# Five side-by-side parts per lane in two row scans, and record clearing moved to the edge layer

## The chip, the core and the metric

The kernel runs on one core of a Trainium2 chip. The metric is the device time of one execution in microseconds, here the median of three runs. The engines are named as in the profile: PE (TensorE), DVE (VectorE), ACT (ScalarE), POOL (GpSimd) and SP (SyncE, which only issues transfers in this kernel).

## What is computed

Four graph layers over 12,500 nodes of 64 features and 400,000 edges, sorted by target node `dst`. Each is `x = x + layer(relu(layernorm(x)))`:

```python
# 0, the edge layer
x_i = x[dst]; x_j = x[src]
h = relu(concat([x_i, x_j - x_i]) @ W1 + b1)
out = segment_max(h @ W2 + b2, dst)          # 0 for a node without edges
# 1: leaky_relu(segment_sum((x * norm_src)[src], dst) * norm_dst @ W + b)
# 2: two hops of a mean over neighbours, each with a matmul of [own, mean]
# 3, the last layer: every edge's row has a weight of its own
message = x[col] * edge_weight[:, None]      # col = dst, row = src
neigh_agg = segment_sum(message, row)
x @ W_self.T + b_self + neigh_agg @ W_neigh.T + b_neigh
```

## The kernel before

**Layout.** The 400,000 sorted edges are split into 128 lanes, one for each partition, of `LANE` = 3125 edges that follow each other. A lane is walked in 125 blocks of `K` = 25 edges. Buffers of five slots (`R` = 5) hold five blocks, and one turn of a hardware loop handles five.

**Edge layer** (the loops over `body0`, from 619 us to 8264 us of the span). For each block:

- SP loads the indices of a later block (`index_load`, line 642), the keys (lines 649 to 651) and the block's rows of `first_rows` (`load_fill`, line 939). `first_rows` has a node's row where its first edge stands, and zeros elsewhere. SP does so in `pass_index` when the block before has been scanned (semaphore `scanned`).
- POOL gathers `x_j` rows with 25 indirect transfers (line 636), one for each column of the block, 128 rows each. It waits for the indices alone and is four to five blocks ahead of DVE.
- DVE makes one-hot matrices of keys (line 685, 20 a block, of which 16 come in pairs for `v` = 0 to 7, the others before them), for PE's counting products. Between them stand single steps of two scans over the 25 columns, each column 128x64 (line 1395, `scan_steps`). The **fill** repeats a node's row over its edges: `fill[j] = fill[j-1]*keep + fill[j]`. The **max** scan takes the running maximum: `ring[j] = max(min(ring[j-1], mask), product[j])`, with the product in a PSUM bank of eight columns. Each step of a scan waits for the one before it. The fill of block b+1 goes on beside the max of block b. After the scan comes the sum of gathered and filled rows (line 1426).
- PE turns the block's rows (line 1928), multiplies them by the second weight (line 1953, semaphore `products0`), and does the counting products (line 1898): first `hist_counts`, 25 pairs of matmuls with no wait among them, then 16 a `v`.
- ACT copies the turned rows and the counts out of PSUM (lines 1755, 1739), and issues the stores of counts (784 KB) and edge rows (800 KB) of the block.

**Three dense sums** (`dense_*`, layers 1 and 2) multiply the stored counts with the nodes' rows, 31 groups each. Beside each group but the first, ACT issues a store of zeros to `records`, the last layer's table (88 stores of 1960 KB, 173 MB in all).

**Last layer** (`body4`, 12,049 us to about 16,775 us), for each of 125 blocks:

- DVE copies the masks (line 691), runs the fill scan over 25 columns, now from SBUF into PSUM banks (line 1630), works out where each message goes in `records` (lines 1638 to 1652), and splits the messages into bf16 planes with ACT (lines 1657, 1662). It then gives `targets`.
- ACT multiplies each filled column by the edge's weight (line 1835) and makes the high and middle planes (1839, 1844). It writes into one of three message buffers, once the scatters that read it last are done.
- PE adds up 25 one-hot matrices for the next block's positions (line 1898, tile kp).
- POOL scatters the 25 columns of messages (line 1181), 128 rows each. It waits for `targets`.
- SP loads first rows, keys and weights five blocks ahead (lines 939 and 1092).

Then 220 units read `records` back and sum them, and the output is written. Small pieces stand between the stages: `place_nodes` works out each node's first and last edge, `first_rows_gpsimd` scatters nodes' rows to `first_rows` and reads one row for each lane's first edge, and `fix_vector`/`fix_gpsimd` carry the maximum over lane borders.

## Time and profile before

| | us |
|---|---|
| median of 3 runs (lowest, highest) | 17606.11 (17545.68, 17622.48) |
| the profiled execution | 17562.39 |
| its span | 17560.6 |
| edge layer's blocks, 619 to 8264 | 7645 |
| last layer's blocks, 12,049 to 16,775 | 4726 |

Busy shares of the span are 44% for PE, 51% for DVE, 34% for ACT and 41% for POOL. No engine is busy throughout, so what a stage costs must be read from that stage. The profiled execution stands 44 us under the median. In a trace row, the first number is the start in us, the second the duration in us, and square brackets hold the idle time of that engine ahead of the row and what ended it.

### The profile page before, as it was taken

The numbers are of one execution on the slowest core, as the hardware profiler recorded it, in microseconds if no ns is written. First come the engines' busy times: TensorE is split into PE (matmuls) and PEld (weight loads), VectorE is DVE, ScalarE is ACT, GpSimd is POOL, SyncE is SP. The second block draws the span as 40 slices with busy tenths as digits, with TensorE's granted clock in tenths as the row PEclk, the third lists the DMA queues.
The fourth block names the chain that finished last, engine by engine and source line by source line (L and its number), as shares of the span: only waits on it lengthen the run. The fifth ranks groups of instructions, "written<-read, shape, count | busy, mean of one in ns | idle before, by whom it ended". The sixth has DMA issues, their size and how long they took to land. (4 is left out here: it accounts for less than half of the span.)

```text
span 17560.6 us, 235099 instructions
## 1 busy us (share of the span) xinstructions
PE 7737.4 (44%) x71916; PEld 5437.9 (31%) x71916; DVE 9024.9 (51%) x17849; ACT 5959.3 (34%) x10705; POOL 7168.5 (41%) x7069
## 2 busy tenths in 40 slices
PE   1244444444444444444697999992000000000045
PEld 1233333333333333333354555551000000000045
DVE  4355555555555555556444443434555555555565
ACT  0122222222222222222576777772222222222211
POOL 4434334343443433333211111115666666666610
PEclk9755555555555555555898998995555555555588
DMA  7222222222222222222585886881111111111177
GB/s 279 89 69 69 69 69 73 66 73 71 69 69 69 69 69 69 69 69 76 183 264 188 253 264 194 262 255 55 56 54 57 55 56 55 57 57 57 51 251 242
DMA packets 1287056, 1982.88 MB, mean 113 GB/s; under 512 B 257381, under 2 KB 1004742, under 8 KB 1281561
## 3 DMA queue, kind: packets, MB, share of 16 engines
q1 hardware_dynamic: 886377, 1080.50, 20.1%
q10 hardware_dynamic: 174288, 612.09, 9.2%
q0 software_dynamic: 225664, 281.41, 5.7%
q8 instruction: 358, 5.87, 0.1%
q14 instruction: 369, 3.02, 0.1%
HBM read 1171.31 MB, written 815.77 MB: 113 GB/s over the span
## 5 line engine op out<-in xcount | busy, mean ns | idle before, releaser
L636 POOL DMA_INDIRECT RF<-tab_edge_b,idx x3125 | 3076.1, 984 | 4638.8 <-DMA idx<-e_src 3636.2
L685 DVE TENSOR_TENSOR HM<-iota_b,eqw 128x2048 bf16<-128x2048 bf16 x2000 | 2192.3, 1096 | 3318.4 <-remote 2902.3
L1181 POOL DMA_INDIRECT records<-RF,idx x3125 | 3094.3, 990 | 1678.8 <-issue 1064.8
L1898 PE MATMUL bk<-HM 128*128 128x98 bf16 x16000 | 1642.8, 254 | 2720.0 <-ACT X L1739 1176.6
L1739 ACT ACTIVATE X<-bk 128x392 uint8<-128x392 f32 x4000 | 1779.8, 495 | 1504.9 <-PE bk L1898 1438.2
L1898 PE MATMUL kp<-HM,ident_b 128*128 128x98 bf16 x3125 | 275.2, 282 | 4473.6 <-issue 2420.2
L1898 PEld LDWEIGHTS bk<-HM 128*128 128x128 bf16 x16000 | 1152.7, 119 | 3253.2 <-issue 3170.6
L769 PE MATMUL tp<-HM,RF 128*64 128x512 bf16 x12276 | 1977.4, 379 | 4.2 <-ACT HM L728 2.6
L876 POOL DMA_INDIRECT agg<-RF,lastT x372 | 537.5, 1445 | 2887.7 <-ACT RF L808 2796.9
L1898 PEld LDWEIGHTS kp<-HM,ident_b 128*128 128x128 bf16 x3125 | 251.6, 142 | 4498.1 <-issue 4498.1
L1755 ACT ACTIVATE hT<-tp 128x512 f32<-128x512 f32 x500 | 255.7, 511 | 3619.2 <-remote 2939.6
L775 PE MATMUL om<-HM,RF 128*64 128x512 bf16 x6138 | 1326.3, 379 | 0.0
L769 PE MATMUL tp<-RF 128*64 128x512 bf16 x5952 | 1011.3, 381 | 226.9 <-ACT RF L728 226.9
L1953 PE MATMUL om<-w_diag,hT 128*128 128x128 f32 (+1 forms) x3250 | 846.5, 400 | 442.0 <-issue 434.5
L769 PEld LDWEIGHTS tp<-HM,RF 128*64 128x64 bf16 x12276 | 813.7, 110 | 632.1 <-issue 72.4
L1395 DVE SCALAR_TENSOR_TENSOR RF<-RF,dupjunk 128x64 f32<-128x64 f32 x3124 | 876.8, 281 | 27.3
L1953 PEld LDWEIGHTS om<-w_diag,hT 128*128 128x128 f32 (+1 forms) x3250 | 711.2, 298 | 535.2 <-issue 510.7
L1395 DVE SCALAR_TENSOR_TENSOR RF<-RF,dupjunk,om 128x64 f32<-128x64 f32 x3124 | 860.4, 275 | 0.4
L730 DVE CAST HM<-dst_f 128x4096 bf16<-128x4096 uint8 x186 | 427.0, 2296 | 727.3 <-DMA dst_f<-counts 401.1
L1630 DVE SCALAR_TENSOR_TENSOR tp<-tp,mblk,RF 128x64 f32<-128x64 f32 x1875 | 549.0, 293 | 468.5 <-DVE tp L1630 255.2
L728 ACT ACTIVATE RF<-dst_f 128x4096 bf16<-128x4096 uint8 x186 | 672.7, 3617 | 331.7 <-PE tp L769 330.6
L728 ACT ACTIVATE HM<-dst_f 128x4096 bf16<-128x4096 uint8 (+1 forms) x186 | 702.2, 3822 | 46.6 <-PE tp L769 46.6
(362 smaller groups left out, 14990.4 us busy)
## 6 DMA issues: line engine op xcount, KB each, us to landing
dst_f<-counts SPq DMA_DIRECT2D x465, 512.0 KB
RF<-first_rows SPq DMA_DIRECT2D x250, 800.0 KB
counts<-X ACTq DMA_DIRECT2D x250, 784.0 KB
records<-RF ACTq DMA_DIRECT2D x88, 1960.0 KB
RF<-records SPq DMA_DIRECT2D x220, 784.0 KB, 5.0
crow<-counts SPq DMA_DIRECT2D x279, 512.0 KB
first_rows<-RF ACTq DMA_DIRECT2D x25, 4000.0 KB
edge_rows<-RF ACTq DMA_DIRECT2D x125, 800.0 KB
```

The costliest lines, as they stand in the source:

```text
L636: e.indirect_dma_start(out=ring[:, r, j, :], out_offset=None, in_=table[:, :], in_offset=bass.IndirectOffsetOnAxis(ap=idx[:, r, j:j + 1], ...
L685: return e.tensor_tensor(to[:, 0:n, :].rearrange("p k (q h) -> p k q h", h=2), iota_b[:, 0:m].rearrange("p (q h) -> p q h", h=2).unsqueeze ...
L728: e.activation(to, of, ACT.Copy).then_inc(sem("widened_A"), 1)
L769: last = e.matmul(tp[u][k * D:(k + 1) * D, :], hi_mid[:, t, k * D:(k + 1) * D], part, start=t == 0, stop=t == TILES - 1, skip_group_check= ...
L775: return e.matmul(om[u][k * D:(k + 1) * D, :], low[:, t, :], part, start=t < 2, stop=t >= TILES - 2, skip_group_check=True)
L876: e.indirect_dma_start(out=agg[:, :], out_offset=bass.IndirectOffsetOnAxis(ap=lastT[:, g * GB + k:g * GB + k + 1], axis=0), in_=out_rows[g ...
L1181: e.indirect_dma_start(out=records[:, :], out_offset=bass.IndirectOffsetOnAxis(ap=idx2[:, r, j:j + 1], axis=0), in_=msgs[MSG_OF[r]][:, j, ...
L1395: e.scalar_tensor_tensor(out=buf[:, r, j, :], in0=prev, scalar=mask[:, j:j + 1], in1=this, op0=op0, op1=op1).then_inc(sem(chain.name), 1)
L1630: loop_chain(e.scalar_tensor_tensor(out=in_bank(j), in0=prev, scalar=mblk[:, 0, j:j + 1], in1=fill[:, r, j, :], op0=ALU.mult, op1=ALU.add))
L1739: e.activation(staged[u].rearrange("p (r k) -> p r k", k=P)[:, :, k:k + 4], bk[s % 2][:, 0:4 * TILES].rearrange("p (k r) -> p r k", k=4), ...
L1898: return e.matmul(to, by_q, by_r, start=start, stop=stop, skip_group_check=True)
L1953: last = e.matmul(om[q % 2][:, k * P:k * P + m], hT[0:m, q % 2, k * P:(k + 1) * P], w_diag[0:m, 0:m], start=True, stop=True)
```

## The change

**Parts.** Each lane's 3125 edges are seen as five parts (`VL` = 5) of 625, and a block now takes five columns of each part in place of 25 columns that follow each other. Position `c*5 + v` of a block is column c of part v, so the five rows of one `c` belong to five separate walks. One instruction of 320 elements does a scan step for five positions:

```python
# fill, in the edge layer and, with mblk, in the last layer
e.copy_predicated(columns(fill, r, c), bcast(mask c), earlier_columns(fill, r, c))
# max
e.scalar_tensor_tensor(out=kept, in0=earlier_columns(ring, r, c), scalar=1.0,
                       in1=bcast(mask), op0=ALU.mult, op1=ALU.min)
e.tensor_tensor(ring[:, r, a:z, :], kept[...], om[q % 2][...], ALU.max)   # a piece per PSUM bank
```

A fill of a block is 5 instructions (25 before), a max is 5 + 8 (25 before; the pieces end where a bank of eight columns ends). In the last layer the fill stays in SBUF, and ACT reads it there:

```diff
-                    for q, cols in enumerate(FILLQ):
-                        wait(e, "highs", b * NF + (q + 1 - NF + 3 * NGROUPS))
...
-                        for j in cols:
-                            prev = in_bank(j - 1) if j else in_bank(K - 1)
...
-                            loop_chain(e.scalar_tensor_tensor(out=in_bank(j), in0=prev, scalar=mblk[:, 0, j:j + 1],
-                                                              in1=fill[:, r, j, :], op0=ALU.mult, op1=ALU.add))
...
+                    for c in range(JJ):
+                        if not (isinstance(b, int) and b + c == 0):
+                            loop_chain(e.copy_predicated(columns(fill, r, c), bcast(mblk[:, 0, c * VL:(c + 1) * VL].bitcast(i32)),
+                                                         earlier_columns(fill, r, c)))
...
-                            last = e.activation(msg_bank(q)[:, j - cols[0], :], in_bank(j), ACT.Copy, scale=wblk[:, r, j:j + 1])
+                            last = e.activation(msg_bank(q)[:, j - cols[0], :], fill[:, r, j, :], ACT.Copy, scale=wblk[:, r, own(j):own(j) + 1])
```

SP's load of a later fill slot in the last layer now also waits for `filled4` of the next block, which reads the slot's last five columns.

**Order on DVE in the edge layer.** The waits for `products0` move from ahead of a pair of one-hots to the first instruction that reads the bank, and the fill and max steps are spread anew:

```diff
                 for h in range(2):
                     for _ in hist_batch(b, h):
-                        several(filling, 2)
+                        several(filling, 1)
                 for _ in count_batch(b, r, 0):
-                    several(filling, 2)
-                for q, cols in enumerate(MAXQ):
-                    wait(e, "products0", b * NQ + (q + 1))
-                    gate(e)
-                    taking = scan_steps(max_chain, ring, b, r, masks[:, r, 1, :], ALU.min, ALU.max, cols, om[q % 2])
-                    for v in range(2 * q + 1, min(2 * q + 3, VB)):
-                        for _ in count_batch(b, r, v):
-                            several(taking, 1)
-                            several(filling, 1)
-                            several(taking, 1)
...
+                    several(filling, 1)
+                taking = max_steps(b, r)
+                for v in range(1, VB):
+                    for _ in count_batch(b, r, v):
+                        several(taking, 1)
+                several(taking, K)
```

**Loads in runs of five.** The indices, and in the last layer the keys and weights, lie in five runs of five numbers (20 bytes) a lane, not in one run of 25 (100 bytes):

```diff
-            e.dma_start(idx[:, r, :], src_l[:, bass.ds((i * R + r) * K, K)])\
+            e.dma_start(by_part(idx[:, r, :]), by_part(src_l)[:, :, bass.ds((i * R + r) * JJ, JJ)])\
...
-                        e.dma_start(to[:, r, :], of[:, bass.ds(b * K, K)]).then_inc(sem(f"first{r}"), 16)
+                        e.dma_start(by_part(to[:, r, :]), by_part(of)[:, :, bass.ds(b * JJ, JJ)]).then_inc(sem(f"first{r}"), 16)
```

**Clearing.** The stores of zeros leave ACT's dense groups. SP issues them behind each block's loads in the edge layer, 120 of 128x10x280 numbers (1400 KB) and four of 128x8x280:

```diff
                 for r in range(R):
                     pass_index(e, i, r)
                     load_fill(e, 0, i, r)
+                    clear_records(e, (i * R + (r - R)) * CLEAR_ROWS + (R - 1) * CLEAR_FIRST, CLEAR_ROWS)
...
-                if not isinstance(g, int) or g > (0 if l == 0 else 1):
-                    e.dma_start(records_flat.rearrange("(p c w) -> p c w", p=P, w=CLEAR_COLS)
...
```

**Small pieces.** `row_numbers` turns edge numbers into the new row order (7 operations on 128x98, called twice). The row for a lane's start and the repair at borders are done for five parts: five indirect transfers where one stood (twice in `first_rows_gpsimd`, twice in `fix_gpsimd`), and 12 more short DVE operations in `fix_vector`.

**DVE's order in the edge layer**, from the first one-hots of a `v` with its fill and max steps. RF holds the ring and the fill, dupjunk the masks, om the products, eqw the keys, HM the one-hots. Before:

```order
L685 TENSOR_TENSOR HM<-iota_b,eqw 128x2048 [waits products0,histed]
L1395 SCALAR_TENSOR_TENSOR RF<-zero_row,dupjunk,om 128x64
L1395 SCALAR_TENSOR_TENSOR RF<-RF,dupjunk 128x64 [waits v_fill]
L1395 SCALAR_TENSOR_TENSOR RF<-RF,dupjunk,om 128x64 [waits v_max]
L685 TENSOR_TENSOR HM<-iota_b,eqw 128x1568
L1395 SCALAR_TENSOR_TENSOR RF<-RF,dupjunk,om 128x64 [waits v_max]
L1395 SCALAR_TENSOR_TENSOR RF<-RF,dupjunk 128x64 [waits v_fill]
L1395 SCALAR_TENSOR_TENSOR RF<-RF,dupjunk,om 128x64 [waits v_max]
```

The same place in the changed kernel (pivots is the buffer of `kept`):

```order
L698 TENSOR_TENSOR HM<-iota_b,eqw 128x2048 [waits histed]
L1473 SCALAR_TENSOR_TENSOR pivots<-RF,dupjunk 128x320
L698 TENSOR_TENSOR HM<-iota_b,eqw 128x1568
L1486 TENSOR_TENSOR RF<-pivots,om 128x320 [waits products0,v_max]
L698 TENSOR_TENSOR HM<-iota_b,eqw 128x2048 [waits banked]
L1473 SCALAR_TENSOR_TENSOR pivots<-RF,dupjunk 128x320 [waits v_max]
L698 TENSOR_TENSOR HM<-iota_b,eqw 128x1568
L1486 TENSOR_TENSOR RF<-pivots,om 128x192 [waits v_max]
```

Behind each one-hot stood three steps of two scans, and now stands one of one scan; the wait for the products is one one-hot pair later.

**DVE's order in the last layer**, from a block's masks to the positions. Before:

```order
L691 COPY mblk<-keep 128x25
L1630 SCALAR_TENSOR_TENSOR tp<-tail,mblk,RF 128x64 [waits v_loop,first1,highs]
L1630 SCALAR_TENSOR_TENSOR tp<-tp,mblk,RF 128x64 [waits v_loop] x7
L1630 SCALAR_TENSOR_TENSOR tp<-tp,mblk,RF 128x64 [waits v_loop,highs]
L1630 SCALAR_TENSOR_TENSOR tp<-tp,mblk,RF 128x64 [waits v_loop] x7
L1630 SCALAR_TENSOR_TENSOR om<-tp,mblk,RF 128x64 [waits v_loop,highs]
L1630 SCALAR_TENSOR_TENSOR om<-om,mblk,RF 128x64 [waits v_loop] x7
L1630 SCALAR_TENSOR_TENSOR tail<-om,mblk,RF 128x64 [waits v_loop,highs]
L1638 CAST rtwice<-rblk 128x50 [waits v_loop]
```

In the changed kernel:

```order
L1699 COPY_PREDICATED RF<-mblk,RF 128x320 [waits v_loop,first1]
L1699 COPY_PREDICATED RF<-mblk,RF 128x320 [waits v_loop] x4
L1707 CAST rtwice<-rblk 128x50 [waits v_loop]
L1710 TENSOR_TENSOR hT<-rtwice 128x625 [waits v_loop]
L1712 TENSOR_TENSOR hT<-hT,eqw 128x625 [waits v_loop]
```

A chain of 25 dependent instructions with four waits for ACT has become a chain of five with none.

**SP's order in the edge layer**, one block of the loop in the changed kernel:

```order
L655 DMA idx<-e_src 128x5x5
L661 ISA
L661 TENSOR_LOAD chunk
L661 ISA x2
L662 ISA
L662 DMA crow<-kr 128x256
L663 ISA
L663 DMA rel<-rel_lin 128x128
...
L958 DMA RF<-first_rows 128x1600
L1010 ISA
L1010 DMA records<-pivots 128x10x280
```

The index load keeps its place and has five runs a lane; the store of zeros stands last.

## Rows read from the trace of the kernel before

**Rows 1.** Busy time by stretch: us, PE, PEld, DVE, ACT, POOL, clock, DMA share, GB/s.
```profile
619.00:8264.00 7645.00, 3603.20 (x27859) 2783.10 (x27859) 4112.70 (x9473) 2074.73 (x4621) 2990.03 (x3038) 0.57 0.22 69
8480.00:9512.00 1032.00, 1027.93 (x9326) 580.42 (x9322) 417.67 (x215) 807.41 (x276) 172.93 (x120) 1.00 0.83 259
12049.00:16775.00 4726.00, 274.21 (x3115) 250.80 (x3116) 2594.97 (x5240) 1177.68 (x4246) 3070.15 (x3100) 0.50 0.18 55
```
**Rows 2.** Timeline of POOL, one block's gathers and the next block's first.
```profile
4003.49 0.95 POOL L636 DMA_INDIRECT RF<-tab_edge_b,idx  x1 [29.65 <-DMA idx<-e_src]
...
4033.80 0.94 POOL L636 DMA_INDIRECT RF<-tab_edge_b,idx  x1 [0.30 <-issue]
4067.97 0.94 POOL L636 DMA_INDIRECT RF<-tab_edge_b,idx  x1 [33.22 <-DMA idx<-e_src]
```
**Rows 3.** Timeline of PE in that block: counting pairs and turns.
```profile
4014.42 0.25 PE L1898 MATMUL mixed<-HM,ident_b 128*128 128x98 bf16 x1
...
4038.87 0.37 PE L1928 MATMUL tp<-ident,RF 128*128 128x128 f32 x1 [0.84 <-issue]
```
**Rows 4.** Timeline of DVE in that block.
```profile
4039.09 1.23 DVE L685 TENSOR_TENSOR HM<-iota_b,eqw 128x2048 bf16<-128x2048 bf16 x1 [24.88 <-remote]
4040.23 0.60 DVE L1395 SCALAR_TENSOR_TENSOR RF<-RF,dupjunk 128x64 f32<-128x64 f32 x2
4040.75 0.97 DVE L685 TENSOR_TENSOR HM<-iota_b,eqw 128x1568 bf16<-128x1568 bf16 x1
...
4043.49 0.28 DVE L1395 SCALAR_TENSOR_TENSOR RF<-RF,dupjunk,om 128x64 f32<-128x64 f32 x1
...
4044.07 0.97 DVE L685 TENSOR_TENSOR HM<-iota_b,eqw 128x1568 bf16<-128x1568 bf16 x1
```
**Rows 5.** Timeline of DVE, the sums of the last two blocks, behind the last gather.
```profile
8195.60 1.82 DVE L1426 TENSOR_TENSOR RF<-RF 128x1600 f32<-128x1600 f32 x1
8230.65 1.82 DVE L1426 TENSOR_TENSOR RF<-RF 128x1600 f32<-128x1600 f32 x1
```
**Rows 6.** Busy time by stretch, inside the block of rows 2.
```profile
4006.00:4016.00 10.00, 6.38 (x48) 5.37 (x49) 6.10 (x16) 1.09 (x2) 7.87 (x8) 0.57 0.94 342
4018.00:4034.00 16.00, 2.67 (x11) 1.05 (x10) 0.00 (x0) 0.00 (x0) 12.04 (x14) 0.50 0.12 27
```
**Rows 7.** Groups of instructions by line and shape: busy us, mean ns.
```profile
L431 DVE SCALAR_TENSOR_TENSOR HM<-HM,stat_rstd 128x448 f32<-128x448 f32 x56 | 35.0, 625 | 7.9 <-remote 2.8 <-DVE stat_rstd L430 2.8 <-issue 0.6
L1524 DVE COPY_PREDICATED X<-HM 128x448 f32<-128x448 int32 x14 | 9.2, 657 | 2.0 <-DVE HM L1523 0.8 <-issue 0.8
L1657 DVE TENSOR_TENSOR om<-om,RF 128x512 f32<-128x512 f32 x125 | 87.4, 700 | 29.4 <-issue 21.7 <-DVE idx L1652 7.7
```
**Rows 8.** DMA issues: count, KB each, median us to landing.
```profile
idx<-e_src SPq DMA_DIRECT2D x125, 12.5 KB, 1.7
RF<-records SPq DMA_DIRECT2D x220, 784.0 KB, 5.0
```
**Rows 9.** Timeline of DVE in the last layer, a block with quick fill steps.
```profile
13593.35 2.71 DVE L1647 TENSOR_TENSOR HM<-HM,kp 128x2450 f32<-128x2450 bf16 x1
13604.35 0.34 DVE L1630 SCALAR_TENSOR_TENSOR tp<-tail,mblk,RF 128x64 f32<-128x64 f32 x1 [0.37 <-DVE mblk L691]
...
13613.61 0.20 DVE L1638 CAST rtwice<-rblk 128x50 bf16<-128x50 f32 x1 [0.24 <-issue]
13617.67 2.71 DVE L1647 TENSOR_TENSOR HM<-HM,kp 128x2450 f32<-128x2450 bf16 x1
```
**Rows 10.** The same, the block before it, with slow fill steps.
```profile
13556.62 0.29 DVE L1630 SCALAR_TENSOR_TENSOR tp<-tail,mblk,RF 128x64 f32<-128x64 f32 x1 [0.97 <-DVE mblk L691]
...
13584.86 0.20 DVE L1638 CAST rtwice<-rblk 128x50 bf16<-128x50 f32 x1 [1.81 <-issue]
```
**Rows 11.** Line 1647 in all: duration ns min/median/max, first and last start.
```profile
L1647 DVE TENSOR_TENSOR HM<-HM,kp x125: 2707/2707/2708, 12062.8 to 16770.9; 128x2450 f32<-128x2450 bf16 x125
```
**Rows 12.** POOL's scatters, group by line: busy us, mean ns of one, idle before.
```profile
L1181 POOL DMA_INDIRECT records<-RF,idx x3125 | 3094.3, 990 | 1678.8 <-issue 1064.8 <-DVEq L329 614.0
```

More of the change, by code:

```diff
@@ L22 @@
 BLOCKS = LANE // K
+VL = 5
+JJ = K // VL
+VLEN = LANE // VL
+ROUND = 1.5 * 2.0 ** 23
 ITERS = BLOCKS // R
@@ L49 @@
 RW = 98
[L50 removed]
+CLEAR_COLS, CLEAR_ROWS, CLEAR_FIRST = 280, 10, 8
 MSG_OF = (0, 1, 2, 0, 1)
@@ L886, in fix_tensor, with fix_vector @@
             e.transpose(pb[:, 0:D], carryT[:, 0:P], ident[0:D, 0:D]).then_inc(sem("fix_tensor"), 1)
-        def fix_vector(e, chain, l, op0, op1, row, colc):
-            e.tensor_copy(tail[:, :], ring[:, R - 1, K - 1, :]).then_inc(sem("fix_vector"), 1)
+        def fix_vector(e, chain):
+            last = lambda v: ring[:, R - 1, K - VL + v, :]
+            for v in range(1, VL):
+                chain(e.scalar_tensor_tensor(out=tail[:, :], in0=tail[:, :] if v > 1 else last(0),
+                                             scalar=part["kL"][:, v:v + 1], in1=last(v), op0=ALU.min, op1=ALU.max))
+            e.sem_inc(sem("fix_vector"), 1)
@@ new lines, in fix_vector @@
+            for v in range(1, VL):
+                chain(e.scalar_tensor_tensor(out=carried[:, v, :], in0=carried[:, v - 1, :], scalar=part["kL"][:, v - 1:v],
+                                             in1=last(v - 1), op0=ALU.min, op1=ALU.max))
+            e.wait_ge(sem("fix_read"), 16 * VL)
+            for v in range(VL):
+                chain(e.scalar_tensor_tensor(out=fixrow[:, v, :], in0=carried[:, v, :], scalar=part["contL"][:, v:v + 1],
+                                             in1=fixrow[:, v, :], op0=ALU.min, op1=ALU.max))
@@ L1067, in _ @@
                 load_fill(e, 0, 0, r)
+            e.wait_ge(sem("zero_tile"), 1)
+            for r in range(R - 1):
+                clear_records(e, r * CLEAR_FIRST, CLEAR_FIRST)
             with e.Fori(1, ITERS) as i:
@@ new lines, in _ @@
+            chain(e.tensor_tensor(part["cont"][:, :], part_starts, part["prev"][:, :], ALU.is_equal))
+            chain(e.tensor_scalar(part["whole"][:, :], part["cnt"][:, :], float(VLEN), None, ALU.is_equal))
+            chain(e.tensor_tensor(part["whole"][:, :], part["whole"][:, :], part["cont"][:, :], ALU.mult))
+            chain(e.tensor_tensor(col["k"][:, :], part["whole"][:, 0:1], part["whole"][:, 1:2], ALU.mult))
+            for v in range(2, VL):
+                chain(e.tensor_tensor(col["k"][:, :], col["k"][:, :], part["whole"][:, v:v + 1], ALU.mult))
```

234 lines of the change are left out of this document (139 added, 95 removed).

## The prediction

> **What bounds the kernel now.** I read the busy time by stretch first, then the timelines of single blocks, since no engine is busy throughout [rows 1]. Three stages matter, and each has a limit of its own.
>
> *Edge layer.* 7645 us for 125 blocks are 61.2 us a block, and no engine is busy for 60% of it [rows 1]. POOL's gathers start at 4003.49 and the last is issued at 4033.80, a burst of 30.3 us; the next burst starts at 4067.97, after 33.22 us of waiting for indices, which SP loads only when DVE has scanned a block [rows 2]. So POOL waits for DVE. DVE in turn waited 24.88 us, up to 4039.09, for PE and ACT [rows 4]. PE was within its 25 counting pairs at 4014.42 and needed until 4038.87 for the rest and the block's turn, though nothing that it waited for shows [rows 3]. In 16 us it started 11 matmuls, while the transfers kept only 12% of the DMA engines busy [rows 6]. What I call **slow issue** is this: the engine is free, its data is there, and instructions come one by one, about 16 / 11 = 1.5 us apart. It ends about 5 us after POOL's last gather, with the turn at 4038.87. Behind the last burst there is none, and a block takes 8230.65 - 8195.60 = 35.05 us, not 61 [rows 5]. A block is thus a front as long as POOL's burst and some 5 us, set off by the index load, and a back of some 25 us that DVE mostly bounds.
>
> *Dense sums.* PE is busy for 1027.93 of 1032 us at full clock [rows 1].
>
> *Last layer.* A block takes (16770.9 - 12062.8) / 124 = 37.97 us [rows 11]. It is made of two sorts of block. With quick steps it takes 24.32 us from one line 1647 to the next, of which the fill takes 13613.61 - 13604.35 = 9.26 us [rows 9]. In the block before, the same fill took 28.24 us, 13556.62 to 13584.86 [rows 10]: slow issue again, beside POOL's scatters. POOL itself needs 25 x (0.990 + 0.30) = 32.2 us a block and was idle for 1678.8 us [rows 12]; 0.30 us of that idle time stands before each scatter.
>
> **The change part by part.** The sum is against the profiled execution, 17562 us.
>
> *Last layer's fill: -590 us.* 25 dependent steps go, 5 come. A predicated copy of 448 elements takes 657 ns, a step of 64 about 290 ns [rows 7, 9]; by the line between them, 320 elements take 535 ns, and with 0.03 us between them five take 2.8 us. A quick block falls from 24.3 to 24.3 - 9.3 + 2.8 = 17.8 us. In a slow block I charge each step the pace of the slow ones, 28.24 / 25 = 1.13 us, on top of little work of its own, so at most 5 x (1.13 + 0.25) = 7 us in place of 28. Such a block takes some 46 us now and would take 25. Both are under POOL's 32.2 us, so POOL becomes the bound, and DVE waits for it instead (through ACT, which waits for a message buffer). Bounds: 32.2 us a block, -5.8 x 125 = -720 us; and nothing, if slow issue spreads over all blocks once POOL never rests. I take 33.2 us, near POOL's floor, because either sort of block is well under it: -4.75 x 125 = -594 us. ACT's 25 weightings now read SBUF; ACT is busy for 1177.68 / 125 = 9.4 us a block in all [rows 1], so even at twice that it lies beside POOL's 32.
>
> *Edge layer's scans: -375 us.* In the back of a block stood 4 fill steps in pairs, 0.52 us a pair (4040.23 to 4040.75), and 14 groups of a max, a fill and a max, each 4044.07 - 4043.49 = 0.58 us [rows 4]: 1.04 + 8.1 = 9.1 us. The other eight fills lie in the front, which is hidden. Now the back has one fill (0.45 us), five minimum steps and eight maximum pieces. The step of 448 elements takes 625 ns, and one of 512 with PSUM 700 ns [rows 7]. Scaled to 320 and with the overlap of 0.09 us that successive rows show [rows 4], five are 5 x 0.40 = 2.0 us; the pieces cover 1600 elements in all, 1600/512 x 0.61 + some 0.06 x 8 = 2.4 us. That is 4.9 us, so DVE saves 4.2 us. PE and ACT work in step with DVE there, through the banks of counts, and may be close behind it, so I take 3.0 us of it; bounds 1 and 4.2, that is -125 to -525 us.
>
> *Index load: +200 us.* It has 640 runs of 20 bytes and not 128 of 100, and every block's front starts with it. It lands 1.7 us after issue; 784 KB in 512 runs land in 5.0 us [rows 8]. At the 342 GB/s of a busy stretch [rows 6] the bytes of the latter are 2.3 us, so 384 more runs cost 1.0 us, and 512 more 1.3 us; small runs are less even, so I take 1.7 us x 120 = 204 us. Bounds: 0, and all of 3.3 us for 384 runs, 4.4 us for 512, 530 us. The Trainium skill ("DMA: Bandwidth & Descriptors", Measured) gives about 10.5 ns for each packet as a floor; by that 512 more are 5.4 us, and the sum would be 440 us worse. The trace speaks against so much, since 512 runs with 784 KB of data land within 5.0 us in all, and no row here has a load of 640 runs.
>
> *Clearing in the edge layer: +0 us.* 1.43 MB more a block are 4.2 us at 342 GB/s [rows 6]. They are issued last by SP, behind the index load, and the busy stretch of transfers ends near 4016 today, 18 us ahead of POOL's last gather [rows 2, 6]. That burst is the cover; if the stores hold up the gathers' data or the fetch of instructions by their whole length, they cost 4.2 x 124 = 520 us. A gain cannot be excluded: PE's slow issue might start later.
>
> *Clearing out of the dense sums: 0 us.* PE waits for nothing there [rows 1].
>
> *Small pieces: +25 us.* 16 more indirect transfers at 1.29 us [rows 12] are 21 us; some 35 short DVE operations at 0.2 to 0.3 us are 9 us, part of it beside other work. Bounds 10 and 50 us.
>
> Sum: -594 - 375 + 204 + 25 = -740 us, so 16,822 us for the profiled execution. It stood 44 us under the median; I forecast **16,870 us** for the median.
>
> **The rivals.**
>
> *Slow issue takes the last layer's gain.* It seems tied to POOL's work, and a POOL that never rests leaves no quick blocks. PE's 25 pairs, ACT's 50 instructions and DVE's remaining 20 all need issue. For it: in a slow block 25 steps took three times their time. Against it: the parts of the block with long operations, from line 1647 to the fill, take about as long in slow blocks. If a block keeps 36.5 us, the last layer gives 185 us and the total is 17,230 us. If in addition the index load costs its upper bound, nothing is left of it: 17,560 us, no change.
>
> *The edge layer's front grows (slower).* The index load and the stores of zeros both lengthen the front, which every block pays. Without an other change, (594 + 375 - 25) / 125 = 7.6 us more a block eat all gains. At the upper bounds, 4.4 + 4.2 = 8.6 us; should the stores also stretch slow issue by as much again, 12.8 us. That is 17,560 + 5.2 x 125 = 18,210 us, at the middle of this case 17,900. The share of 94% of the DMA engines in the first 10 us [rows 6] speaks for it; the quiet 18 us behind it speak against.
>
> *Slow issue in the edge layer gives way.* If it starts 4 us later because bulk transfers last 4 us longer, PE has done its counting before it, and the front no longer needs the burst's end. A block could fall towards the 35.05 us of rows 5, at most to POOL's 32 us. A fifth of that way, 5 us, gives 16,240 us; half of it 15,250 us. Nothing in the rows shows why it starts, so I can't exclude it.
>
> *The change does little:* the counts of instructions are as stated, but DVE isn't what the back waits for, and ACT or PE is. Then the edge layer loses 200 us by the index load and the last layer pays for it only in part: 17,500 us.
>
> **How the numbers follow.** Chances: forecast 0.50; slow issue takes the gain 0.17 (of it 0.12 at 17,230 and 0.05 at no change); front grows 0.15 (0.02 of it within 0.5%); edge layer gives way 0.10; little effect 0.08. A measurement of this kernel can tell about 0.5%, 88 us, from no change. Faster by more: 0.50 + 0.12 + 0.10 + 0.02 = 0.74. Within: 0.05 + 0.02 + 0.06 = 0.13. Slower: 0.13. The range of the forecast itself comes from its bounds, 16,500 to 17,250. To leave out no more than 2 in 10 it takes in part of the second and the fourth case: 16,300 to 17,450.
>
> **What would show it.** In the last layer: line 1699 at some 0.53 us, POOL's scatters with little idle time but the 0.30 us, line 1717 each 33 us. In the edge layer: blocks of about 59.5 us; index load landing in 3 to 3.5 us; the wait before the first one-hot of `v` = 0 still over 20 us; the minimum step at 0.49 us. In the dense sums: 33 us a group as now, with a lower DMA share. The forecast is wrong if the last layer's blocks stay over 36 us, if edge blocks are longer than 61.2 us, or if the wait of 24.88 us has gone.

## The result, and the profile after

| | before | changed |
|---|---|---|
| median, us | 17603.28 (4 runs, 17545.68 to 17622.48) | 16603.31 (4 runs, 16570.32 to 16657.12) |
| ratio | | 0.9438, 95% interval 0.9411 to 0.9465 |
| profiled execution | 17562.39 | 16657.12 |

The change saves 1000 us in the median, and 905 us between the two profiled executions, since the profiled one before lies 41 us under its median and the one after 54 us over it. The forecast was 16,870 us with a range from 16,300 to 17,450, so the time lies in the range, 267 us under the forecast. Its two large terms are both wrong, though, and they err in opposite directions. That shows as soon as the profile is read stage by stage.

Busy time by stretch of the changed kernel, edge layer and last layer (columns, and the rows of the kernel before: [rows 1]):

```profile
619.00:7440.00 6821.00, 3311.91 (x27859) 2687.39 (x27859) 3655.90 (x5496) 2108.01 (x4620) 3159.39 (x3047) 0.60 0.33 104
11200.00:15840.00 4640.00, 275.16 (x3125) 251.59 (x3125) 2037.35 (x2742) 1252.41 (x4247) 3054.31 (x3087) 0.50 0.21 57
```

The sum that ends each edge block (first row; before: 619.3 to 8230.6) and the step that marks each last-layer block (second row; before: [rows 11]), first and last start:

```profile
L1506 DVE TENSOR_TENSOR RF<-RF x125: 1814/1818/1822, 624.9 to 7411.2; 128x1600 f32<-128x1600 f32 x125
L1717 DVE TENSOR_TENSOR HM<-HM,kp x125: 2706/2707/2708, 11215.9 to 15832.7; 128x2450 f32<-128x2450 bf16 x125
```

From these starts every piece of the span follows:

| piece | before | changed | difference |
|---|---|---|---|
| up to the first edge block | 619.3 | 624.9 | +6 |
| edge layer, 124 blocks | 7611.3 (61.4 a block) | 6786.3 (54.7 a block) | -825 |
| between (dense sums) | 3832.2 | 3804.7 | -27 |
| last layer, 124 blocks | 4708.1 (38.0 a block) | 4616.8 (37.2 a block) | -91 |
| to the end of the span | 789.7 | 822.7 | +33 |
| sum | 17560.6 | 16655.4 | -905 |

The forecast had -375 + 204 = -171 us for the edge layer and -594 us for the last one.

**Last layer.** Groups of DVE and POOL in the stretch from 11,200 to 15,840 us: the fill, the one-hot that follows it, the scatters.

```profile
L1699 DVE COPY_PREDICATED RF<-mblk,RF 128x320 f32<-128x320 int32 x624 | 325.1, 521 | 86.6 <-DMA wblk<-e_weight 18.6 <-issue 12.8 <-DVE mblk L704 10.4
L698 DVE TENSOR_TENSOR HM<-iota_b,rtwice 128x2450 bf16<-128x2450 bf16 x125 | 179.4, 1435 | 1685.3 <-remote 1639.7 <-issue 37.0 <-DVE inrank L1713 8.4
L1208 POOL DMA_INDIRECT records<-RF,idx x3086 | 3054.1, 990 | 1585.6 <-issue 979.0 <-DVEq L338 606.6
```

The same groups of the kernel before, from 12,049 to 16,775 us (the fill's two largest, the one-hot, the scatters):

```profile
L1630 DVE SCALAR_TENSOR_TENSOR tp<-tp,mblk,RF 128x64 f32<-128x64 f32 x1875 | 549.0, 293 | 468.5 <-DVE tp L1630 255.2 <-issue 114.8 <-remote 38.5
L1630 DVE SCALAR_TENSOR_TENSOR om<-om,mblk,RF 128x64 f32<-128x64 f32 x875 | 256.2, 293 | 505.8 <-DVE om L1630 359.9 <-issue 92.2 <-remote 33.1
...
L685 DVE TENSOR_TENSOR HM<-iota_b,rtwice 128x2450 bf16<-128x2450 bf16 x125 | 179.4, 1435 | 452.1 <-remote 303.2 <-issue 138.7 <-DVE inrank L1643 10.1
...
L1181 POOL DMA_INDIRECT records<-RF,idx x3100 | 3070.1, 990 | 1657.7 <-issue 1057.5 <-DVEq L329 600.1
```

The fill did what was forecast: 521 ns a step (535 was said), and DVE's busy time in the stage fell from 2595 to 2037 us. The idle time ahead of the fill steps is nearly gone: the two groups shown had 974 us of it, and now there are 87. A quick block fell to 18 us, as forecast (17.8). But the idle time ahead of one single instruction, the one-hot behind the fill, went from 452 to 1685 us, 1233 more. POOL stayed idle for nearly as long as before. A stall that had been spread over 25 steps now stands in one place.

The timelines of DVE, PE and POOL show what that place is like:

```profile
13523.68 2.94 DVE L1699 COPY_PREDICATED RF<-mblk,RF 128x320 f32<-128x320 int32 x5 [0.17 <-DVE mblk L704]
...
13528.46 0.81 DVE L1713 TENSOR_REDUCE inrank<-hT 128x25 f32<-128x625 bf16 x1
13572.11 1.44 DVE L698 TENSOR_TENSOR HM<-iota_b,rtwice 128x2450 bf16<-128x2450 bf16 x1 [42.84 <-remote]
...
13507.44 2.20 PE L1969 MATMUL kp<-HM,ident_b 128*128 128x98 bf16 x25 [22.17 <-issue]
13576.49 2.20 PE L1969 MATMUL kp<-HM,ident_b 128*128 128x98 bf16 x25 [66.84 <-DVEq L1718]
...
13568.57 0.97 POOL L1208 DMA_INDIRECT records<-RF,idx  x1 [0.30 <-issue]
```

The one-hot waits for PE's count, which PE makes from what DVE did in the block before. The row of PE's 25 products for it ends at 13509.64, 20 us before DVE came to the wait, and PE did nothing after it. DVE still stood for 42.84 us, until 3.5 us behind the start of the last of POOL's 75 scatters in a row (13568.57; the run of 75 began at 13473.17). Blocks now come mostly in threes of 18, some 25 and 69 us, where most took 24 or some 48 us before. Nor is it a late transfer of instructions: in these 40 us the trace has none, and in the 16 quiet us of [rows 6] none either. In the 69 us block SP's three small loads, between which it waits for nothing, go out 2.9 us apart:

```profile
13533.93 0.70 SPq L1119 DMA_DIRECT2D rblk<-r_lin  x1
13536.85 0.70 SPq L1119 DMA_DIRECT2D qblk<-q_lin  x1
13539.76 0.70 SPq L1119 DMA_DIRECT2D wblk<-e_weight  x1
```

**Edge layer.** Here is where a block's time goes, averaged over 105 blocks of each trace (worked out from the starts of the rows, not a view of the profile), in us from the start of the block's sum (line 1426, now 1506):

```
                                     before  changed
POOL's first gather                    1.9     2.5
POOL's last gather (25th)             32.8    34.8
first one-hot of v = 0                25.5    12.5
                     1                38.1    17.1
                     2                41.5    30.7
                     3                45.3    39.9
                     7                59.4    52.5
the next block's sum                  62.0    55.1
```

Before, v = 1 started 5.3 us behind POOL's last gather. Now v = 3 starts 5.1 us behind it. Two more values of `v`, each 3.55 us before (v = 1 to v = 7 in six steps), are started beside the burst. The five behind it take 3.15 us each in place of 3.55, 2.0 us in all. Against that the front is 2.0 us longer: 0.7 by the index load, 1.3 by slower gathers. -7.1 - 2.0 + 2.0 is -7.1 us, and the table has -6.9. It also shows that v = 0 starts 13 us sooner.

### The profile page after: what moved, and what is told of

Read it like the earlier page. It is cut to its first block and busy times, and to the rows that moved or that the text cites. A ratio compares the mean times of both kernels' runs of the same rounds, so it can differ in the third digit from the quotient of the medians.

```text
span 16655.4 us, 228031 instructions
## 1 busy us (share of the span) xinstructions
PE 7442.4 (45%) x71916; PEld 5270.8 (32%) x71916; DVE 8010.3 (48%) x11391; ACT 6068.0 (36%) x10705; POOL 7332.9 (44%) x7085
## 5 line engine op out<-in xcount | busy, mean ns | idle before, releaser
L645 POOL DMA_INDIRECT RF<-tab_edge_b,idx x3125 | 3236.0, 1036 | 3666.1 <-DMA idx<-e_src 2659.8
L698 DVE TENSOR_TENSOR HM<-iota_b,eqw 128x2048 bf16<-128x2048 bf16 x2000 | 2192.1, 1097 | 2833.1 <-remote 1632.3
L788 PE MATMUL om<-HM,RF 128*64 128x512 bf16 x6138 | 1451.4, 379 | 0.0
L782 PEld LDWEIGHTS tp<-HM,RF 128*64 128x64 bf16 x12276 | 857.1, 110 | 651.7 <-issue 49.0
L698 DVE TENSOR_TENSOR HM<-iota_b,rtwice 128x2450 bf16<-128x2450 bf16 x125 | 179.4, 1435 | 1685.3 <-remote 1639.7
L2024 PE MATMUL om<-w_diag,hT 128*128 128x128 f32 (+1 forms) x3250 | 706.8, 377 | 62.4 <-issue 60.3
L788 PE MATMUL om<-RF 128*64 128x512 bf16 x2976 | 726.5, 381 | 0.0
L741 ACT ACTIVATE HM<-crow 128x4096 bf16<-128x4096 uint8 x186 | 670.4, 3604 | 0.0
L2024 PEld LDWEIGHTS om<-w_diag,hT 128*128 128x128 f32 (+1 forms) x3250 | 637.3, 284 | 93.9 <-issue 75.8
```

The lines of the kernel that those rows point to most:

```text
L645: e.indirect_dma_start(out=ring[:, r, j, :], out_offset=None, in_=table[:, :], in_offset=bass.IndirectOffsetOnAxis(ap=idx[:, r, own(j):own ...
L698: return e.tensor_tensor(to[:, 0:n, :].rearrange("p k (q h) -> p k q h", h=2), iota_b[:, 0:m].rearrange("p (q h) -> p q h", h=2).unsqueeze ...
L741: e.activation(to, of, ACT.Copy).then_inc(sem("widened_A"), 1)
L782: last = e.matmul(tp[u][k * D:(k + 1) * D, :], hi_mid[:, t, k * D:(k + 1) * D], part, start=t == 0, stop=t == TILES - 1, skip_group_check= ...
L788: return e.matmul(om[u][k * D:(k + 1) * D, :], low[:, t, :], part, start=t < 2, stop=t >= TILES - 2, skip_group_check=True)
L2024: last = e.matmul(om[q % 2][:, k * P:k * P + m], hT[0:m, q % 2, k * P:(k + 1) * P], w_diag[0:m, 0:m], start=True, stop=True)
```

## The experiments

The experiments ran on three chips, and that turned out to matter. A ratio is always to the kernel before on the same chip. The changed kernel itself stands beside the experiments on the third chip alone. On the first two its place is taken by the result above (ratio 0.9438, 54.7 and 37.2 us a block), whose own chip is not on record; the kernel before took 17603.28 us there, 17617.26 us on the first chip and 17534.60 us on the second.

### First chip: are the stores of zeros the cause?

With the change, bulk transfers last until about 16 us into POOL's burst and not 12, and slow issue (instructions that come one by one though nothing that they wait for is late) seemed to begin when they end. So theory A was that the stores hold it off.

**The stores moved back to the dense sums:**

```diff
-                    clear_records(e, (i * R + (r - R)) * CLEAR_ROWS + (R - 1) * CLEAR_FIRST, CLEAR_ROWS)
...
+                if not isinstance(g, int) or g > (0 if l == 0 else 1):
+                    clear_records(e, g * 14 + (-1, 28, 57)[l] * 14, 14)
```

> The changed kernel with the stores of zeros moved back: SP stores none in the edge layer, ACT stores 88 of 1960 KB beside the dense groups. The edge layer's block fell from 61.5 us to 55.0 us (medians) with the change. Theory A (transfers hold off slow issue: bulk transfers last until about 17 us into POOL's burst in place of 12, so DVE gets two more v into the front): without the stores the block goes back by the two v, 2 x 3.3 us, and the burst falls by 1 us, so 59 to 61 us a block, total 17,150 to 17,350 us. Theory B (the shorter scans and the wait behind the one-hots do it, the stores cost a little): block 54 us, total 16,450 to 16,600 us. The dense sums stay at 33 us a group in both.

Measured: 16638.62 us, ratio 0.9455 (0.9432 to 0.9477). The edge block takes (7384.4 - 623.5) / 124 = 54.5 us. The stretch between the layers takes 3805.6 us with the stores in it, 3804.7 without them. The block is where theory B had it (54), the total 39 us above its range.

**The same from the other side,** the kernel before with SP's stores in the edge layer, and none in the dense sums:

```diff
-                if not isinstance(g, int) or g > (0 if l == 0 else 1):
-                    e.dma_start(records_flat.rearrange("(p c w) -> p c w", p=P, w=CLEAR_COLS)
...
                     load_fill(e, 0, i, r)
+                    clear_records(e, (i * R + (r - R)) * 10 + (R - 1) * 8, 10)
```

> The kernel before with nothing changed but the stores of zeros: SP issues them behind each block's loads in the edge layer, ACT none in the dense sums. Theory A (transfers hold off slow issue): the pairs of the first counts are done before it starts, v = 0 and v = 1 move into the front; but DVE waits for the products ahead of v = 1 as before, so a part of the gain: block 57 to 59 us, total 17,050 to 17,300 us. Theory B (scans and wait do it): block 61.5 to 63 us, total 17,600 to 17,800 us.

Measured: 17627.04 us, ratio 1.0004 (0.9989 to 1.0019). In the profile the edge block is 60.5 us and not 61.4, and the last layer's 39.3 and not 38.0; the total shows neither. The last layer's code is the same in both, so between two profiles a stage can move by 1.3 us a block without an edit of its own. In this kernel v = 0 starts at 20.5 us, 5 us sooner than in the kernel before, so with the old scans the stores do move the front a little; v = 3 comes 1.2 us sooner. Neither theory's block (57 to 59, 61.5 to 63) was met.

**Twice the stores:**

```diff
                     clear_records(e, (i * R + (r - R)) * CLEAR_ROWS + (R - 1) * CLEAR_FIRST, CLEAR_ROWS)
+                    clear_spare(e, (i * R + (r - R)) * CLEAR_ROWS, CLEAR_ROWS)
```

> The changed kernel with a second store of zeros of 1400 KB behind each block's first in the edge layer, into a table that nothing reads. Theory A: bulk transfers last until about 21 us into the burst, DVE gets one or two more v into the front, block 50 to 53 us, total 16,000 to 16,350 us, unless POOL's burst grows by as much. Theory B: the block is the same or 1 to 4 us longer by the burst, total 16,600 to 17,100 us.

Measured: 16635.22 us, ratio 0.944 (0.9419 to 0.9461), edge block 54.6 us.

**Stores in the last layer:**

```diff
+                    if not isinstance(i, int):
+                        clear_spare(e, (i * R + (r - R)) * CLEAR_ROWS, CLEAR_ROWS)
             loop(e, body4)
```

> The changed kernel with a store of zeros of 1400 KB a block in the last layer, issued by SP behind the block's loads, into a table that nothing reads. The last layer's blocks take 37.2 us, in threes of 18, 24 and 69 us, with DVE waiting up to 42.8 us although what it waits for was done 20 us before. Theory A (bulk transfers hold off slow issue): at least half of the stall goes, blocks 33 to 35.5 us, total 16,100 to 16,400 us. Theory B (slow issue does not depend on bulk transfers, they only cost): blocks 37.2 to 41 us, total 16,600 to 17,100 us.

Measured: 16668.64 us, ratio 0.9456 (0.9417 to 0.9495), last-layer block 37.6 us.

Theory A asked for another time in each of the four, and in none did it come. In the totals, stores of 1400 KB a block cost nothing and give nothing that shows, in either layer, and neither do those of the dense sums. Clearing is worth 0 in both places, as forecast; the end of the bulk transfers does not set where the front ends.

### Second chip: the wait's place, SP's load, POOL's burst

**The wait for the products put back ahead of the one-hots:**

```diff
                 for v in range(1, VB):
+                    if v % 2:
+                        wait(e, "products0", b * NQ + (v + 1) // 2)
+                        gate(e)
                     for _ in count_batch(b, r, v):
```

> The changed kernel with DVE's wait for the products put back ahead of the one-hots of v = 1, 3, 5 and 7, where the kernel before has it; the new scans stay. Of 6.9 us a block that the edge layer gave, two v that DVE now does beside POOL's burst are 7.1, shorter steps about 2, and the longer burst takes 2. Theory W (the wait's place lets DVE go ahead): v = 1 goes back behind the burst, the block back to 58 to 61 us, total 17,000 to 17,350 us. Theory S (the shorter scans alone, with fewer instructions on DVE, do it): block 55 to 56.5 us, total 16,600 to 16,800 us.

**The kernel before with the later wait:**

```diff
-                    wait(e, "products0", b * NQ + (q + 1))
-                    gate(e)
-                    taking = scan_steps(...)
                     for v in range(2 * q + 1, min(2 * q + 3, VB)):
                         for _ in count_batch(b, r, v):
-                            several(taking, 1)
+                            done += 1
+                            if done == 2:
+                                wait(e, "products0", b * NQ + (q + 1))
+                                gate(e)
+                                taking = scan_steps(...)
+                            several(taking, 3)
```

> The kernel before with its old scans of 25 steps, but with DVE's wait for the products behind the one-hots of v = 1, 3, 5 and 7, and the eight maximum steps of a bank behind it in threes. Theory W (the wait's place): v = 1 and one more v in the front, block 56.5 to 59 us, total 17,000 to 17,300 us. Theory S (the scans): block 60.5 to 62 us, total 17,450 to 17,700 us.

**A small load in place of SP's 800 KB in the last layer:**

```diff
-                    load_fill(e, 4, i, r)
...
+                        wait(e, "filled4", i * R + (r - R + 2))
+                        gate(e)
+                        e.dma_start(fill[:, r, 0, :], lrows(first_rows)[:, bass.ds((i * R + r) * K, 1), :]
+                                    .rearrange("p a f -> p (a f)")).then_inc(sem(f"first{r}"), 16)
```

From the sixth block on the other 24 columns of the slot keep old rows, so this kernel scatters other messages and its output is another one.

> The changed kernel, but in the last layer SP loads only the first of a block's 25 columns of first_rows, 32 KB in place of 800 (from the sixth block on; the rest of the slot keeps old rows, so the messages are other ones). In the trace slow issue seemed to begin where SP issues this load. Theory L (the load sets slow issue off): the blocks fall from 37.2 us to 32.5 to 34 us, total 16,000 to 16,250 us. Theory P (slow issue comes with POOL's long bursts of scatters, whatever SP does): blocks 36.5 to 37.5 us, total 16,500 to 16,650 us.

**POOL waits for its scatters behind each block:**

```diff
+                    wait(e, f"moved{r}", i * (16 * K) + (16 * ITERS * K + 16 * K))
+                    gate(e)
             loop(e, body4)
```

> The changed kernel, but in the last layer POOL waits behind each block's 25 scatters until they have landed, 2 to 3 us, before it goes on to the next block. In the trace DVE waits through two of POOL's blocks and comes free 3.5 us behind the last scatter. Theory P (slow issue ends when POOL's queue runs empty, and lasts while it doesn't): DVE comes free once a block, POOL never lacks targets, blocks 34 to 35.5 us, total 16,200 to 16,400 us. Theory Q (the pause is too short to end it, or the restart costs as much): blocks 37 to 40 us, total 16,600 to 17,000 us.

| | us | ratio | edge block | last-layer block |
|---|---|---|---|---|
| new scans, early wait | 17086.53 | 0.9737 (0.9712 to 0.9761) | 56.0 | 38.9, untouched |
| old scans, late wait | 17634.74 | 1.0054 (1.0036 to 1.0071) | 62.5 | 37.7, untouched |
| small load | 16972.09 | 0.967 (0.9635 to 0.9705) | 55.5, untouched | 38.8 |
| POOL waits | 16929.04 | 0.9641 (0.9616 to 0.9666) | 56.2, untouched | 38.3 |

The totals alone mislead here. The three kernels made from the changed one are 2 to 3% slower, against the kernel before, than the changed kernel in the result. A good part of that lies in stages that the edits don't touch: 1.7 us a block in the last layer of the first row, 0.8 and 1.5 us in the edge layer of the other two. The starts that the blocks are worked out from, edge layer of the first, third and fourth row:

```profile
L1506 DVE TENSOR_TENSOR RF<-RF x125: 1816/1819/1822, 624.0 to 7564.4; 128x1600 f32<-128x1600 f32 x125
```
```profile
L1512 DVE TENSOR_TENSOR RF<-RF x125: 1817/1819/1822, 623.3 to 7511.2; 128x1600 f32<-128x1600 f32 x125
```
```profile
L1508 DVE TENSOR_TENSOR RF<-RF x125: 1816/1820/1822, 624.2 to 7591.2; 128x1600 f32<-128x1600 f32 x125
```

So each stage is read against the kernels on the same chip that leave it alone. The two kernels with the same edge layer differ by 0.6 us a block in it, so less than that can't be told apart. The early wait has 56.0 us where the others have 55.5 and 56.2: its place is worth nothing that shows. With the old scans the later wait, with the maximum steps in threes behind it, costs 0.5%.

Theory W falls in both. Theory S is what is left, though its numbers were met only in part (block 56.0 us in its range but total 17086.53 above it and in theory W's, by what the untouched last layer adds; total 17634.74 in its range but block 62.5 above it): what remains of the change in the edge layer gives the time, that is the shorter scans and what came with them, the order of rows in parts and the new spread of the fill steps. With the early wait v = 2 starts at 38.1 us and not at 34.2 as in the run where POOL waits, yet v = 3 starts at 41.9 us in both. DVE's order around the first `v` is therefore not what sets the end.

The traces do show what goes with the scans. In all seven kernels with the new ones on the chips with slow issue, PE starts the last of its 50 counting matmuls of the front at 10.0 us in the median block, and v = 0 starts at 12 to 14 us in the mean. In the three with the old ones that last matmul starts at 12.1 us (10.6 and 12.4 in the two variants) and v = 0 at 25.5 us (20.5 and 27.9). The first of the 50 starts only 0.4 us sooner with the new scans.

In the last layer the small load (38.8 us) is no better than the kernel that leaves that layer alone (38.9). POOL's pause of 2.2 us behind each block gives 38.3 us, no more of a difference than kernels with the same code there have shown, where theory P asked for 34 to 35.5 us. Its total, 16929.04 us, is in theory Q's range; that of the small load is in neither of the two ranges given for it. Neither SP's load nor an unbroken burst of more than 25 scatters explains the stall: with the pause in place, blocks of 60 to 69 us are still there. Both theories on its cause that I had formed from the trace have fallen.

### Third chip: no slow issue at all

The changed kernel was run again here, as a measure for the spread just seen.

> The changed kernel as it is, as a measure for the kernels beside it: in runs of another call, stages whose code was untouched took 55.5 to 56.2 us a block in the edge layer where the changed kernel has 54.7, and 38.3 to 38.9 in the last layer where it has 37.2. If that is the chip, this run shows it too: edge blocks 55.5 us or more, total over 16,750 us. If it is the other kernels' code, this run has 54.7 and 37.2 again, total 16,550 to 16,660 us.

Measured: the kernel before takes 13768.92 us on this chip (7 runs, 13744.33 to 13773.12), the changed one 13476.77 us. That is 3,840 and 3,130 us less than in the result, with the same programs; the ratio is 0.9794 (0.9778 to 0.981). Neither expectation had room for it. Starts of the two markers in the changed kernel on this chip:

```profile
L1506 DVE TENSOR_TENSOR RF<-RF x125: 1811/1818/1845, 569.2 to 4897.9; 128x1600 f32<-128x1600 f32 x125
L1717 DVE TENSOR_TENSOR HM<-HM,kp x125: 2706/2707/2708, 8673.2 to 12641.3; 128x2450 f32<-128x2450 bf16 x125
```

Its groups by line:

```profile
L645 POOL DMA_INDIRECT RF<-tab_edge_b,idx x3125 | 3473.2, 1111 | 992.0 <-issue 951.9 <-DMA tab_edge_b<-HM 33.1 <-DMA idx<-e_src 6.9
L1208 POOL DMA_INDIRECT records<-RF,idx x3125 | 3108.8, 995 | 979.0 <-issue 979.0
L698 DVE TENSOR_TENSOR HM<-iota_b,eqw 128x2048 bf16<-128x2048 bf16 x2000 | 2179.4, 1095 | 214.6 <-PE mixed L1969 75.2 <-DVE RF L1486 69.0 <-PE bk L1969 17.6
L698 DVE TENSOR_TENSOR HM<-iota_b,rtwice 128x2450 bf16<-128x2450 bf16 x125 | 179.3, 1435 | 22.0 <-DVE inrank L1713 21.8
```

Two of these groups in the changed kernel's profile of the result:

```profile
L645 POOL DMA_INDIRECT RF<-tab_edge_b,idx x3125 | 3236.0, 1036 | 3666.1 <-DMA idx<-e_src 2659.8 <-issue 915.5 <-DMA tab_edge_b<-HM 90.8
L698 DVE TENSOR_TENSOR HM<-iota_b,eqw 128x2048 bf16<-128x2048 bf16 x2000 | 2192.1, 1097 | 2833.1 <-remote 1632.3 <-PE bk L1969 799.9 <-PE mixed L1969 174.8
```

DVE's one-hots last 1095 ns here and 1097 there (both means are over two sizes, 128x2048 and 128x1568); of the groups shown only the gathers differ, and they are longer here. The time comes from the waits: 215 us ahead of the edge layer's one-hots and not 2833, 22 ahead of the last layer's and not 1685, 6.9 us for indices and not 2660. SP's three small loads go out 0.67 us apart and not 2.9:

```profile
10293.87 0.57 SPq L1119 DMA_DIRECT2D rblk<-r_lin  x1
10294.53 0.59 SPq L1119 DMA_DIRECT2D qblk<-q_lin  x1
10295.21 0.59 SPq L1119 DMA_DIRECT2D wblk<-e_weight  x1
```

So slow issue is not made by this kernel's order of work alone. It belongs to the chip, or to a state that a chip was in: every profile of the result and of the first two chips has it, and on the third chip no profile has it and none of the 21 runs has its time. What the repetition was meant for, whether the spread of untouched stages on the second chip comes from the chip or from where the code lies, is left open by it. Without it POOL bounds both layers. The last layer takes 32.0 us a block by DVE's marker, and POOL needs 25 x (0.995 + 0.31) = 32.6 by the means of its row. Between the first block's first scatter and the last block's it was 32.5 us a block, with no idle time but the 0.3 us before each; DVE's marker shows less because DVE begins 11 us ahead of POOL and ends some 70 us ahead. The edge layer takes 34.9 us, against 25 x (1.111 + 0.30) = 35.3; there POOL has gathered 83 of its 3125 columns before the first marker.

**The three other kernels on this chip** were made for slow issue, and here there was none to test them on. In each the expected totals were those of the slower chips, so none was met. The first makes the three short mask operations of a block three times:

```diff
                     masks_of(nb, nr)
+                    masks_of(nb, nr)
+                    masks_of(nb, nr)
```

> The changed kernel with the three short mask operations of a block made three times in place of once, which puts about 1.3 us of work on DVE ahead of the block's first one-hots, at the head of the front. Theory H (a head start decides: what PE and DVE get done before slow issue begins, about 11 us behind POOL's first gather, is quick, what is left costs 0.7 us an instruction; the change won by a head start of 1 us): PE has 8 or more of its 25 pairs left, v = 0 and v = 1 fall back, block up by 2.5 to 5 us, total 16,900 to 17,250 us. Theory O (POOL's burst covers the front, so 1.3 us more of it cost nothing): block up by 0 to 1.3 us, total 16,600 to 16,770 us.

Measured: 13476.93 us, ratio 0.9793 (0.9776 to 0.9809), edge block 34.9 us as in the changed kernel. With POOL as the bound, 1.3 us more on DVE are covered. Theory H is neither borne out nor refuted by this, since its condition was absent.

The second moves four fill steps of a block behind the one-hots of the first counts:

```diff
                     for _ in hist_batch(b, h):
-                        several(filling, 1)
+                        pass
...
-                    for _ in count_batch(b, r, v):
+                    for n, _ in enumerate(count_batch(b, r, v)):
+                        if v < 4 and n == 0:
+                            several(filling, 1)
                         several(taking, 1)
```

> The changed kernel with the four fill steps beside the one-hots of the first counts moved behind them: two beside v = 0 as two of them are now, three beside v = 1 to 3. That gives DVE and PE 1.6 us more of a head start and puts 0.4 to 0.8 us more behind the burst. Theory H: v = 1 to 3 come earlier, block 52 to 54 us, total 16,250 to 16,500 us. Theory O: block 55 to 55.8 us, total 16,600 to 16,700 us.

Measured: 13618.36 us, ratio 0.9899 (0.9883 to 0.9916), 142 us slower than the changed kernel, with an edge block of 36.1 us and not 34.9. POOL's row tells where:

```profile
L645 POOL DMA_INDIRECT RF<-tab_edge_b,idx x3125 | 3622.3, 1159 | 990.4 <-issue 952.2 <-DMA tab_edge_b<-HM 33.2 <-DMA idx<-e_src 4.9
```

A gather takes 1159 ns and not 1111: 25 x 0.048 = 1.2 us a block, the whole loss. DVE's work is the same, only its order differs, so on this chip POOL's gathers become longer by when DVE does its work beside them.

The third gathers 13 of a block's 25 columns from the sixth block on; the other 12 keep old rows, so its output is another one:

```diff
-            for j in range(K):
+            for j in range(K if isinstance(i, int) else G):
                 e.indirect_dma_start(out=ring[:, r, j, :], out_offset=None, in_=table[:, :],
```

with `G = 13`, and the waits on `moved` adapted.

> The changed kernel, but from the sixth block on POOL gathers 13 of a block's 25 columns in the edge layer; the other 12 columns of the slot keep what they held, so their rows are other ones. POOL's burst falls from 32.3 to 16.8 us. Theory G (slow issue lasts from some 11 us into the gathers to 5 us behind the last one): the front ends at 2.5 + 16.8 + 5 = 24 us, six v at 3.2 us follow, block 41 to 46 us, total 14,900 to 15,600 us. Theory N (what holds the front up is another thing, POOL's burst only runs beside it): block 50 to 55 us, total 16,000 to 16,650 us.

Measured: 13144.63 us, ratio 0.9548 (0.9529 to 0.9567), edge block (4564.9 - 569.8) / 124 = 32.2 us. On this chip it shows what lies under POOL's bound: with half the gathers the block falls by 2.7 us only, and DVE is then busy for 3600 us of 4011 (569 to 4580 us), POOL for 1789. So DVE's own work, with its waits for PE and ACT, is close behind POOL's. Theory G, on the front in slow issue, stays untested.

## Why the prediction came out as it did

**The total, in the range.** It came out by luck, through two errors against each other: 500 us too much in the last layer, 650 too little in the edge layer. By the prediction's own signs its account is wrong: it names last-layer blocks over 36 us (37.2) and the end of the 24.88 us wait (v = 0 starts at 12.5 us, not 25.5). Of the smaller signs, the predicated copy (0.52 us) and the minimum step (0.48 us) came as said; edge blocks (54.7 us, not 59.5) and the index load (2.3 us, not 3 to 3.5) did not.

**Last layer's fill, -594 forecast, -91 measured.** The step that failed: "Such a block takes some 46 us now and would take 25". Slow blocks take up to 69 us instead. I had charged slow issue to the instructions that it was seen on, 1.13 us for each of 25 steps. The trace after shows that it isn't bought by the step. With the steps gone, the idle time ahead of them fell by 887 us (974 to 87) and that ahead of the next instruction rose by 1233, with 42.84 us in one wait whose condition had long been met. Counted in matmuls alone, as in the prediction, slow issue in the edge layer is 1.5 us apart; with the 10 weight loads of the same stretch [rows 6] it is 16 / 21 = 0.76 us an instruction. My first rival, which had 36.5 us a block, described this; it is what happened in that stage (37.2). What makes instructions come slowly stays open. Its total of 17,230 us lacks the 44 us between the profiled execution and the median that the forecast has. POOL's floor itself was forecast well: where slow issue is absent, the stage runs at 32.0 us a block, and the forecast's bound was 32.2. Whether the old fill would run at the same 32 us there, its 24.3 us being shorter too, is likely by the quick blocks of [rows 9]. That is argued and not shown, for no profile of the kernel before was taken on that chip.

**Edge layer's scans, -375 forecast.** The step that failed: "The other eight fills lie in the front, which is hidden". The price of the back was near the truth: behind the burst a `v` became 0.4 us cheaper. But the front isn't a fixed cover. Two more `v`, 7.1 us a block, moved into it, and v = 0 begins at 12.5 us and not at 25.5. I found the cause by elimination alone: it isn't the stores (three runs) and not the place of the wait (two runs), so it is the scans and what is with them. The order in parts and the spread of the fill steps were not tested apart from the shorter scans. Why shorter scans let v = 0 start 13 us sooner I had explained by a head start of about 1 us. The traces agree with it: PE begins the last of its 50 counting matmuls at 10.0 us in the median block and not at 12.1. But the cause was argued only, and the run made to test it met a chip without slow issue. It stays open.

**Index load, +204 forecast, about +80 measured.** The page of the changed kernel has 2.3 us from issue to landing, where [rows 8] has 1.7 us:

```profile
idx<-e_src SPq DMA_DIRECT2D x125, 12.5 KB, 2.3
```

512 more runs cost 0.6 us, 1.2 ns each, and POOL's first gather comes 0.7 us later. At the floor of about 10.5 ns a packet that the Trainium skill gives ("DMA: Bandwidth & Descriptors", Measured, for transfers issued from GpSimd) they would have cost 5.4 us by estimate; for this load, issued from SP, the trace has 0.6 us. Of the front's growth I had missed the larger part, 1.3 us by the gathers, 1037 ns each in the edge layer and 985 before.

**Clearing, 0 forecast in both places.** Right, and shown from both sides.

**Small pieces, +25 forecast, +11 measured** by the table (+6, -27 and +33 before rounding; why the end takes 33 us longer was not looked into).

## What to carry to other kernels

When instructions come slowly though nothing that they wait for is late, do not charge the delay to the instructions on which it shows: with them gone, 1233 us more of idle time stood ahead of the next one. Read a result by stage even where the total agrees with the forecast, and compare a stage with kernels on the same chip that leave it alone, since untouched stages took up to 5% longer on the second chip here than in the result. And run the kernel on another chip before you build on a theory of its stalls: what looked like a property of the schedule on two chips was absent on the third.

## What the hardware showed that was not expected

- The same two programs took 17,600 and 13,770 us on different chips (before), 16,600 and 13,480 us (changed), each within 0.6% from run to run on one chip. The gain is 5.6% on the one and 2.1% on the other.
- With slow issue SP's issues of small loads are 2.9 us apart and not 0.67, beside unchanged durations of DVE's one-hots (1097 and 1095 ns) and POOL's last-layer scatters (990 and 995 ns).
- A gather on POOL took between 985 and 1159 ns in the mean: 985 with the old scans and 1037 with the new ones in the traces before and after, 1111 and 1159 on the third chip for two orders of the same DVE work. The Trainium skill ("SBUF — State Buffer", SBUF: two separate sides) describes a port pair that DVE and GpSimd take turns on. That could be what lengthens them; no run here isolates it.
